# A gated recurrence on one Trainium2 core: the last sixteen steps reordered

## The reference

```
vz, vr, vh = video @ C_z + b_z, video @ C_r + b_r, video @ C + b
xz, xr, xh = seq @ W_z, seq @ W_r, seq @ W        # for all time steps
def step(h, (xzt, xrt, xht)):
    z  = sigmoid(xzt + h @ U_z + vz)              # update gate
    r  = sigmoid(xrt + h @ U_r + vr)              # reset gate
    hh = tanh(xht + (r * h) @ U + vh)             # candidate
    return (1 - z) * h + z * hh
x = x + layer1(x, cond_1024);  x = x + layer2(cond_1024, x)
```

## Time and profile before

| | |
|---|---|
| median of 3 runs | 1593.68 us |
| the profiled execution's own time | 1593.41 us |
| its span | 1591.5 us |
| TensorE busy | 1569.3 us, 99% of the span |
| VectorE, ScalarE, GpSimd busy | 1347.6, 835.3, 228.7 us |
| chain that ended last | TensorE 95%, VectorE 2%, issue 1%, ScalarE 1% |

### The profile page before, as it was taken

The page is one execution under the profiler, slowest core; times in us unless marked ns, Lnnn a source line. Parts: engine busy times, 40 slices in busy tenths (PEclk is TensorE's granted clock), DMA queues, the critical chain, the costliest instruction groups (busy, mean ns, idle before and its releaser), DMA issues.

```text
span 1591.5 us, 47642 instructions
## 1 busy us (share of the span) xinstructions
PE 1569.3 (99%) x20030; PEld 1220.6 (77%) x20030; DVE 1347.6 (85%) x3158; ACT 835.3 (52%) x1868; POOL 228.7 (14%) x284
## 2 busy tenths in 40 slices
PE   9999999999999999999999999999999999999997
PEld 6888888888888767777777777777777777777887
DVE  5888889899877888888898888888988888889776
ACT  5999999999888843333333233333333333333232
POOL 0000000000000011112222211212222222222221
PEclk9999999999999999999999999999999999999999
DMA  6154445433452520110100101101001011000000
GB/s 241 27 141 124 133 99 161 138 80 106 96 167 53 169 100 2 56 55 2 55 29 29 55 2 56 55 2 55 27 30 55 2 55 46 11 29 2 30 30 29
DMA packets 56902, 104.91 MB, mean 66 GB/s; under 512 B 10224, under 2 KB 46576, under 8 KB 47344
## 3 DMA queue, kind: packets, MB, share of 16 engines
q1 hardware_dynamic: 54528, 86.13, 15.5%
q0 software_dynamic: 2160, 15.73, 5.3%
HBM read 65.16 MB, written 36.70 MB: 64 GB/s over the span
## 4 chain that ended last, share of the span: by engine, by line
PE 95%; DVE 2%; issue 1%; ACT 1%; DMA 0%; SPq 0%; DVEq 0%
PE ps L948 33%; PE ps L1002 28%; PE ps L1030 17%; PE ps L1018 15%; PE ps L966 2%; PE ps L921 1%; DVE ST L832 1%; DMA raw<-in_x 0%; DVE ST L879 0%; ACT ST L559 0%; DVE HL L886 0%; PE ps L979 0%; DVE RL L864 0%; DVE XP L799 0%; DVE ST L865 0%
## 5 line engine op out<-in xcount | busy, mean ns | idle before, releaser
L948 PE MATMUL ps<-XS,W 128*128 128x512 f32 x2304 | 525.2, 390 | 2.3 <-ACT XS L406 2.3
L948 PEld LDWEIGHTS ps<-XS,W 128*128 128x128 f32 x2304 | 433.3, 188 | 93.2 <-ACT XS L406 1.7
L1002 PE MATMUL ps<-XB,W 128*128 128x512 f16 (+1 forms) x1584 | 272.4, 321 | 0.0
L1018 PEld LDWEIGHTS ps<-HL,U 128*128 128x128 f16 x6352 | 209.2, 98 | 40.2 <-issue 13.8
L1002 PE MATMUL ps<-AR,W 128*128 128x512 f16 x1008 | 235.8, 379 | 0.0
L1018 PE MATMUL ps<-HL,U 128*128 128x64 f16 x6352 | 224.1, 193 | 11.6 <-DVE HL L886 11.6
L1030 PE MATMUL ps<-HL,U 128*128 128x64 f16 x4064 | 204.9, 204 | 0.0
L1002 PEld LDWEIGHTS ps<-XB,W 128*128 128x128 f16 x1584 | 126.6, 98 | 92.7
L555 ACT ACTIVATE ST<-ST 128x256 f32<-128x256 f32 x127 | 52.9, 417 | 266.9 <-DVE ST L837 237.5
L553 ACT ACTIVATE ST<-ST 128x128 f32<-128x128 f32 x254 | 72.1, 310 | 210.3 <-DVE ST L832 210.2
L1030 PEld LDWEIGHTS ps<-HL,U 128*128 128x128 f16 x4064 | 176.4, 98 | 0.0
(11 more groups left out here) (94 smaller groups left out, 1944.1 us busy)
## 6 DMA issues: line engine op xcount, KB each, us to landing
x_scratch<-AR SPq DMA_DIRECT2D x16, 1024.0 KB, 5.6
AR<-in_xj POOLq DMA_DIRECT2D x15, 1024.0 KB, 8.1
out_y<-raw SPq DMA_DIRECT2D x11, 1024.0 KB, 4.2
raw<-in_x SPq DMA_DIRECT2D x10, 1024.0 KB, 10.0
raw<-x_scratch SPq DMA_DIRECT2D x10, 1024.0 KB, 4.8
ST<-in_x SPq DMA_DIRECT2D x5, 1024.0 KB, 8.4
out_y<-AR SPq DMA_DIRECT2D x4, 1024.0 KB, 5.6
w_scratch<-U SPq DMA_DIRECT2D x3, 1024.0 KB, 8.1
```

The source lines that it names most:

```text
L948: op = pe.matmul(ps[b][:, :], W[:, g, wp, k, e * P:(e + 1) * P], XS[:, c % 2, xp, k, :], start=n == 0, stop=n == 11)
L1002: op = pe.matmul(o, second_weights(W2_ORDER.index(g), wp, k, e), x, start=n == 0, stop=n == 11)
L1018: pe.matmul(ps[b][:, col:col + B], U[:, g, uh, k, e * P:(e + 1) * P], S[:, k, 0], start=opens, stop=False, skip_group_check=True)
```

## The change

Three things are edited. In steps 112 to 127 the reset gate's second part, with the wait for `hlo`, goes ahead of the update gate's first part. Of the projection matmuls of a step 9 stay ahead of the candidate and 32 or 33 go behind it. On VectorE, `evacuate_first` moves behind the update gate's sum, and a bank that is finished behind the candidate is emptied one half in the next step's `evacuate_first` and the other in its `evacuate_second`. The wait of a step for its projection counts one emptied half less where only the first half is needed.

```
-LAST_LOOK = 28
+LAST_LOOK = 9
...
+            return xp_after(number(j, tt // 2, g, KT - 1)) - (1 - tt % 2)
...
+            def complete(items):
+                return [(j, part, g, e) for j, part, g, e, k, wp, xp, n in items if n == 11 and (part is None or e == KT - 1)]
+
             def evacuate_first(t):
+                late = complete(fills_of_step(t - 1)[look(t - 1):]) if t else []
+                for j, part, g, e in [b for b in late if b[1] is not None] + complete(fills_of_step(t)[:look(t)]):
+                    evacuate(j, part, g, e, 0)
+
+            def evacuate_second(t):
+                late = complete(fills_of_step(t - 1)[look(t - 1):]) if t else []
+                for j, part, g, e in late + complete(fills_of_step(t)[:look(t)]):
+                    if part is not None:
+                        evacuate(j, part, g, e, 1)
+                for j, part, g, e in complete(fills_of_step(t)[look(t):]):
+                    if part is None:
                         evacuate(j, part, g, e)
...
-                evacuate_first(t)
                 dve.wait_ge(s_Z, u + 1)
                 add_x(t, zg, Z, 0, (0, 1, 2, 3), s_zh, s_pz, u + 1)
+                evacuate_first(t)
...
-                if joint:
-                    pe.wait_ge(s_hlo, t)
-                    recurrent_second(t, R, 1, HL, s_R)
-                    recurrent_first(t, (Z, Z), 0, HL, None)
-                else:
-                    recurrent_first(t, (Z, Z), 0, HL, None)
-                    pe.wait_ge(s_hlo, t)
-                    recurrent_second(t, R, 1, HL, s_R)
+                pe.wait_ge(s_hlo, t)
+                recurrent_second(t, R, 1, HL, s_R)
+                recurrent_first(t, (Z, Z), 0, HL, None)
                 recurrent_second(t, (Z, Z), 0, HL, s_Z)
```

More of the change, by code:

```diff
@@ L228, in fills_of_step @@
             i, n = t - TC * (NCH - 2), 2 * TC - 2
-            return todo[len(todo) * i // n:len(todo) * (i + 1) // n]
+            return todo[len(todo) * i // n:len(todo) * (i + 1) // n] if i < n else []
         def look(t):
@@ L245, in xp_ready @@
             j, tt = divmod(t, TC)
-            return xp_after(number(j, tt // 2 if j == NCH - 1 else None, g, KT - 1))
+            if j < NCH - 1:
+                return xp_after(number(j, None, g, KT - 1))
+            return xp_after(number(j, tt // 2, g, KT - 1)) - (1 - tt % 2)
         def is_joint(t, g):
@@ L800, in evacuate @@
                                          op0=ALU.mult, op1=ALU.add).then_inc(s_xp, 1)
+            def complete(items):
+                return [(j, part, g, e) for j, part, g, e, k, wp, xp, n in items if n == 11 and (part is None or e == KT - 1)]
             def evacuate_first(t):
-                for j, part, g, e, k, wp, xp, n in fills_of_step(t)[:look(t)]:
-                    if n == 11 and part is None:
-                        evacuate(j, part, g, e)
[L806 to L818, removed]
+                late = complete(fills_of_step(t - 1)[look(t - 1):]) if t else []
[8 more added lines that the diff above has]
+                    if part is None:
+                        evacuate(j, part, g, e)
             def add_x(t, dst, b, g, es, s_high, s_done, count):
@@ L1036, in _ @@
                 fill = fills_of_step(t)
-                joint = t < JOINT
                 u = t - 1
```

## The result

The changed kernel takes 1580.06 us (median of 4 runs, 1579.07 to 1581.03) against 1593.74 (1593.51 to 1594.15). The ratio is 0.9914, 95% interval 0.9897 to 0.9931: 13.7 us faster, clear of noise. The forecast was 1579.5, the range 1578.0 to 1584.5.

What follows compares the result with a forecast made beforehand. It took TensorE's 6.48 us of work and a chain through reset gate, candidate and new state to share each step. 1593.41 less 12.3 + 1.0 + 0.9 = 14.2, plus 0.27, gave 1579.5 us, range 1578.0 to 1584.5.

Steps and rivals of the forecast that it cites:

- S: Start of the candidate's second part, counted from the step's first matmul; forecast 4.23 instead of 5.29, next step 2.06 later.
- The 14 steps: Steps 112 to 125: TensorE's work alone sets the step, 90.9 us against 103.19, 12.3 us less.
- sums at 1.37: Reset gate's sums on VectorE start 1.37 us behind the step's start instead of 2.30.
- the overrun of 0.2: In steps 112 to 125, projection matmuls behind the candidate end 0.2 us behind `hhi`, so TensorE becomes the bound.
- the `hlo` wait: Wait ahead of the reset gate's second part: 0.04 us if the step starts on `hhi`, nothing if TensorE comes late.
- Step 126: Step without projection: next step starts at 5.79 against 6.79, 1.0 us less, with 0.04 lost to the evacuation.
- Step 127 and the tail: Last step: earlier second part and z*tanh, 0.73 + 0.16 = 0.9 us less; the tail behind it stays.
- VectorE's chain as the bound: Rival: chain from S grows by an evacuation's 0.48 us, step 6.77, 3.9 less gain, 1583.4 us; chance 0.13.
- TensorE needs the pause: Rival: feeding instructions gives back 0.35 us a step without pauses, gain 9.3, 1584.4 us; chance 0.04.
- Slower by the weight loads: Rival: 32 projection weight loads in a row behind the candidate take 98 ns each, 1598.4 us; chance 0.03.
- no other work would be late: Against the rival that the candidate waits for something else, steps stay 7.37 and the time is 1591.8 us; chance 0.01.
- The sum 14.2: Whole forecast gain in us: 12.3 for steps 112 to 125, 1.0 for step 126, 0.9 for step 127.

Runs made afterwards that it cites:

- a third left out: Changed kernel without a third of the projection matmuls behind the candidate in steps 112 to 125; one run, 1580.09 us.
- the last bank cut: Changed kernel with the last projection bank's 48 matmuls cut into two sets of 64 columns, one run in step 126's pause, evacuations placed anew; 1580.02 us.

## Why the prediction was right

The runs stand here side by side; the usual step is the one that most of the 14 take. S is worked out as in the prediction, with 0.13 for the `hlo` stall where the step starts on `hhi` in the new order:

| order, ahead, evacuations | S | S + 2.06 | usual step | 14 steps |
|---|---|---|---|---|
| old, 28, old (before) | 5.29 | 7.35 | 7.35 | 103.19 |
| new, 28, new | 5.42 | 7.48 | 7.49 | 104.87 |
| new, 18, new | 4.86 | 6.92 | 6.93 | 97.19 |
| old, 9, old | 4.50 | 6.56 | 6.79 | 95.89 |
| old, 9, new | 4.50 | 6.56 | 6.79 | 95.35 |
| new, 9, new, a third left out | 4.36 | 6.42 | 6.43 | 90.18 |
| new, 9, new (changed kernel) | 4.23 | 6.29 | 6.49 | 90.96 |
| new, 9, old | 4.23 | 6.29 | 6.49 | 90.96 |
| new, 0, new | 3.73 | 5.79 | 6.49 | 91.34 |

Where S + 2.06 is the longer, it is the step. Where it is not, the step is TensorE's work, 6.49, with a stall ahead of the candidate in the old order that the numbers of S give as 0.27 (4.50 - 4.23) and the steps as 0.30.

**The 14 steps.** Forecast 12.3 less, measured 103.19 - 90.96 = 12.2. The terms were right one by one: sums at 1.37, S at 4.23, projection 55.7 ns a matmul, the overrun of 0.2 that covers the chain, and the `hlo` wait free under it. The parts don't add: 9 ahead alone gives 7.3, the new order with the moved evacuations and 28 ahead loses 1.7, all together gives 12.2. The new order with the old evacuations and 28 ahead was not run; the 1.7 is 13 times the `hlo` stall that the rows show.

**Step 126.** Forecast 1.0 less, measured 6.79 - 6.03 = 0.76. This term was mis-sized. S was 3.73 as said, but the evacuation ahead of the candidate's sums was priced at the 0.39 of a next instruction on VectorE. These sums read what it writes, and wait for its end: 0.57. The experiment with that evacuation moved takes 0.17 back.

**Step 127 and the tail.** Forecast 0.9, measured 10.33 - 9.54 = 0.79: the 10.33 runs from 1581.17 in the earlier trace rows to the span's end of 1591.5. The `hlo` wait was priced at 0.04 from a wait on `rlo`; it cost 0.13 to 0.14, as in each step that starts on `hhi`: the second part starts at 1.07, not at 0.97. Priced so, the new order with 28 ahead could have been seen to lose.

**The rivals.** *VectorE's chain as the bound* did not come, but the margin is thin: the bare chain in its stalled form, 6.42, is 0.07 below TensorE's work, and not the 0.2 of the prediction. With the last bank cut, TensorE's work fell below it in every second step and part of the stall came back. *TensorE needs the pause* was wrong as a steady cost; 14 steps ran without a gap in both profiles of the changed kernel. Gaps of 0.3 to 0.4 us did come singly in four other kernels (18 ahead, none ahead, a third left out, the last bank cut). *Slower by the weight loads* is refuted by 33 late matmuls in 1.84 us, 55.8 ns each. The Trainium skill's 81 ns ("TensorE: Matmul & The Clock Gate", section "Back-to-back issue gap"), which the prediction set against its sum, does not hold for these pairs either. The prediction's 1593.9 for it has all 41 matmuls of a step at 81 ns (4.20 + 41 x 0.081 = 7.52, an estimate with the page's figure), which is beyond the 7.37 of before and not just short of it as the sentence says. That no other work would be late is shown by the window, TensorE busy 90.96 of 90.96.

The sum 14.2 against 13.78 measured in the stretch is off by 0.24 in step 126, 0.11 in step 127 and the tail, and 0.07 in the 14 steps.

## What to carry to other kernels

Write a step as two lengths, the busiest engine's own work and the chain that returns to its start, and work out both for each edit. Two edits that shorten the chain at different places are worth their sum only if neither still waits for what the other removes: freeing the reset gate earlier paid only once the candidate no longer stood behind 28 matmuls. Put filler work where its engine would wait, until it just outlasts the wait; there more of it, or a tidier order on a second engine, is worth nothing.

## What the runs showed of the hardware beyond that

At `hhi` and at `hlo` a TensorE matmul started 0.14 to 0.15 us behind the end of the VectorE instruction that it waited for (`hlo`: 1547.13 to 1547.28). At `rlo` it was 0.06 us, and not only in the trace of before (two steps): it is 0.06 in each of the 16 steps in both kernels with the old order and 9 ahead (in step 121 above, `rlo` ends at 1536.77 and the matmul starts at 1536.83). In the code two semaphore waits stand directly ahead of the reset gate's second part and one ahead of the candidate's; whether that makes the difference was not tested, and the cause is open.

TensorE's stream of some 2,590 matmuls ran without a gap in four profiles, and with single gaps in others, put down to issue in the rows (0.37 us in the kernel with none ahead, 0.4 in the one with the last bank cut). No run here tells what causes them.
